# A transformer layer on eight cores: the second LayerNorm's rows turned into columns by DMAs instead of TensorE

## What is computed

```python
x = x + attn(layernorm(x))        # 16 heads of 128; causal; out @ out_w.T + out_b
x = x + ffn(layernorm(x))

def ffn(x):                       # gate_w, up_w: 2048 x 6144, down_w: 6144 x 2048, rounded to fp8
    gate = silu((x @ gate_w) * gate_scale)
    up = (x @ up_w) * up_scale
    return ((gate * up) @ down_w) * down_scale

def layernorm(x):
    return (x - mean(x)) / sqrt(var(x) + 1e-5)
```

## Time and profile before

| | us |
|---|---|
| median of 3 runs (1669.6 to 1670.41) | 1670.07 |
| the profiled execution | 1671.04 |
| its span on the slowest core (the cores: 1663.9 to 1669.5) | 1669.5 |
| TensorE busy | 1581.0 |
| VectorE busy | 477.4 |
| ScalarE busy | 377.7 |
| granted TensorE clock, mean | 0.995 |

### The profile page before, as it was taken

The page is one execution under the profiler, slowest core; times in us unless marked ns, Lnnn a source line. Parts: engine busy times, 40 slices in busy tenths (PEclk is TensorE's granted clock), DMA queues, the critical chain, the costliest instruction groups (busy, mean ns, idle before and its releaser), DMA issues.

```text
span 1669.5 us, 23252 instructions; the slowest of 8 cores (1663.9 to 1669.5 us)
## 1 busy us (share of the span) xinstructions
PE 1581.0 (95%) x8897; PEld 779.7 (47%) x9034; DVE 477.4 (29%) x1053; ACT 377.7 (23%) x508; POOL 65.9 (4%) x128
## 2 busy tenths in 40 slices
PE   3788999999998999999999999999999999999998
PEld 2544555555555544444444444444444444444444
DVE  5564455445445566111111111111111111111111
ACT  3453555555556311100000000000000000000000
POOL 0000000000000000000000000000000000000000
PEclk9899999999999999999999999999999999999999
DMA  9624325112143772535365646564444091939210
GB/s 301 173 72 77 61 51 96 20 30 33 20 68 65 114 214 89 101 31 45 33 56 47 53 37 54 49 52 38 38 39 38 1 109 55 98 79 106 79 52 29
DMA packets 33099, 117.15 MB, mean 70 GB/s; under 512 B 3744, under 2 KB 6112, under 8 KB 28128
## 3 DMA queue, kind: packets, MB, share of 16 engines
q0 software_dynamic: 17856, 58.73, 35.1%
q1 hardware_dynamic: 15136, 56.93, 10.5%
HBM read 233.08 MB, written 16.78 MB: 150 GB/s over the span
## 4 chain that ended last, share of the span: by engine, by line
PE 89%; DVE 4%; DMA 3%; issue 2%; ACT 1%; SPq 0%; DVEq 0%; ACTq 0%
PE PS L1083 20%; PE PS L1063 20%; PE PS L1069 20%; PE PS L890 7%; PE PS L1045 6%; PE PS L975 3%; PE PS L899 3%; PE PS L909 3%; PE PS L854 3%; PE PS L953 3%; DMA X<-xq 2%; PE PS L835 1%; DMA RES<-xq 1%; PE PS L934 1%; DVE ONa L600 1%
## 5 line engine op out<-in xcount | busy, mean ns | idle before, releaser
L1063 PE MATMUL PS<-X2T,W 128*128 128x512 bf16 x1506 | 344.9, 379 | 2.7 <-DVE RES L644 1.1
L1069 PE MATMUL PS<-X2T,W 128*128 128x512 bf16 x1505 | 344.9, 379 | 1.6
L696 DVE SCALAR_TENSOR_TENSOR FUSE<-PS,CF,SIL 128x512 bf16<-128x512 f32 x96 | 72.1, 751 | 589.8 <-PE PS L1069 581.3
L1063 PEld LDWEIGHTS PS<-X2T,W 128*128 128x128 fp8e4 x1536 | 150.1, 98 | 182.3 <-issue 1.5
L1069 PEld LDWEIGHTS PS<-X2T,W 128*128 128x128 fp8e4 x1536 | 150.3, 98 | 181.2
L771 ACT ACTIVATE P<-PS,NEGB 128x1024 bf16<-128x1024 f32 x192 | 172.3, 900 | 139.6 <-PE PS L953 137.0
L820 ACT ACTIVATE SIL<-PS,CF 128x512 bf16<-128x512 f32 x96 | 65.9, 687 | 584.7 <-PE PS L1063 584.7
L1083 PE MATMUL PS<-WDa,FUSE 128*128 128x512 fp8e4 x768 | 166.1, 379 | 1.2 <-DVE FUSE L696 1.2
L1083 PE MATMUL PS<-WDb,FUSE 128*128 128x512 fp8e4 x768 | 166.1, 379 | 0.0
L890 PE MATMUL PS<-XQT,WQ 128*128 128x512 bf16 x500 | 131.2, 379 | 0.9
L1083 PEld LDWEIGHTS PS<-WDa,FUSE 128*128 128x128 bf16 x768 | 75.0, 98 | 92.1 <-issue 1.7
(11 more groups left out here) (128 smaller groups left out, 1058.0 us busy)
## 6 DMA issues: line engine op xcount, KB each, us to landing
W<-gu POOLq DMA_DIRECT2D x48, 512.0 KB, 9.5
X<-xq SPq DMA_DIRECT2D x8, 1024.0 KB, 10.3
X<-xo SPq DMA_DIRECT2D x8, 1024.0 KB, 5.5
WQ<-wq POOLq DMA_DIRECT2D x16, 512.0 KB, 6.6
WO<-wo POOLq DMA_DIRECT2D x16, 512.0 KB, 10.0
RES<-xq SPq DMA_DIRECT2D x8, 1024.0 KB, 13.9
res_scr<-RES SPq DMA_DIRECT2D x8, 1024.0 KB, 5.5
RB<-res_scr SPq DMA_DIRECT2D x32, 256.0 KB, 4.4
```

The source lines that it names most:

```text
L696: e.scalar_tensor_tensor(FUSE[:, io * 1024 + qb * 512:io * 1024 + qb * 512 + 512], bank(2 * (f % 3) + 1), USC[:, io:io + 1], SIL[f % 3][:, ...
L1063: mm = e.matmul(bank(2 * (f % 3)), W8[io % 4][:, c * 128:(c + 1) * 128], X2T[:, c * 1024 + qb * 512:c * 1024 + qb * 512 + 512], start=(c = ...
L1069: mm = e.matmul(bank(2 * (f % 3) + 1), W8[io % 4][:, 2048 + c * 128:2048 + (c + 1) * 128], X2T[:, c * 1024 + qb * 512:c * 1024 + qb * 512 ...
```

## The change

The 16 groups of transposes into banks 6 and 7, ScalarE's copies of them, and their place in the list of banks go. The sync queue issues one transposing DMA for each tile, XH2 (128 x 2048, bf16) straight into X2T, when VectorE has written XH2, with a semaphore for each of the two buffers (`d_turn`). Its list is rewritten: four RES loads first, then for each tile the write to res_scr, the transposing DMA, and for the first four tiles a wait for that write and the load of RES for tile t + 4. VectorE waits for `d_turn` before it overwrites an XH2 buffer. FFN job 0 waits for 30 adds and for the turns of tiles 0 to 3, job 1 for 32 adds, job 2 for all turns. The down projection begins at 92 products, asks for 94 at the 47th matmul of its first output tile, and for 96 at its fifth.

```diff
--- before.py
+++ after.py
@@ -236,6 +236,7 @@
     d_idb = sem("d_idb")
     d_outb = sem("d_outb")
     d_dsc = sem("d_dsc")
+    d_turn = [sem("d_turn0"), sem("d_turn1")]
     d_wkva = [sem(f"d_wkva{i}") for i in range(4)]
     d_wq = [sem(f"d_wq{i}") for i in range(3)]
     d_wk = [sem(f"d_wk{i}") for i in range(2)]
@@ -307,7 +308,6 @@
             order += [(job, 6 + job[2] % 2 if job[0] == "P" else 6 if job[0] in "QNXY" else 7)
                       for job, lo, _ in st if lo == 0]
     order += [(("P", 0, 2), 6), (("P", 0, 3), 7), (("O", 15, 1), 6)]
-    order += [(("T", 16 + t, half), 6 + half) for t in range(8) for half in range(2)]
     BANK = dict(order)
     assert len(BANK) == len(order)
     BEFORE = {}
@@ -395,25 +395,25 @@
             load_x(n)
         e.wait_ge(v_latt, 16)
         e.dma_start(out=OUTB[:, :], in_=A(outb_d, 0, [[0, 128], [1, 2048]])).then_inc(d_outb, 16)
-        for t in range(8):
-            if t < 2:
-                e.wait_ge(t_q, count(("Q", 15, 1)))
-                e.wait_ge(t_k, count(("K", 15, 3)))
-            elif t < 4:
+        def load_res(t):
+            e.dma_start(out=RES[t % 4][:, :], in_=xq_d.ap()[t * 128:(t + 1) * 128, :]).then_inc(d_r[t % 4], 16)
+
+        e.wait_ge(t_q, count(("Q", 15, 1)))
+        e.wait_ge(t_k, count(("K", 15, 3)))
+        for t in range(4):
+            if t == 2:
                 e.wait_ge(t_av, 192)
                 e.wait_ge(t_o, 32)
-            else:
-                e.wait_ge(d_spill[t % 4], 16 * (t // 4))
-                e.wait_ge(v_xh, 16 + t - 3)
-            e.dma_start(out=RES[t % 4][:, :], in_=xq_d.ap()[t * 128:(t + 1) * 128, :]).then_inc(d_r[t % 4], 16)
-            if t >= 2:
-                e.wait_ge(v_add, 4 * (t - 1))
-                e.dma_start(out=res_d.ap()[(t - 2) * 128:(t - 1) * 128, :],
-                            in_=RES[(t - 2) % 4][:, :]).then_inc(d_spill[(t - 2) % 4], 16)
-        for t in range(6, 8):
+            load_res(t)
+        for t in range(8):
             e.wait_ge(v_add, 4 * (t + 1))
-            e.dma_start(out=res_d.ap()[t * 128:(t + 1) * 128, :],
-                        in_=RES[t % 4][:, :]).then_inc(d_spill[t % 4], 16)
+            e.dma_start(out=res_d.ap()[t * 128:(t + 1) * 128, :], in_=RES[t % 4][:, :]).then_inc(d_spill[t % 4], 16)
+            e.wait_ge(v_xh, 16 + t + 1)
+            e.dma_start_transpose(out=A(X2T, t * 128, [[16384, 128], [1024, 16], [1, 128]]),
+                                  in_=XH2[t % 2][:, :]).then_inc(d_turn[t % 2], 16)
+            if t < 4:
+                e.wait_ge(d_spill[t % 4], 16)
+                load_res(t + 4)
         for i in range(4):
             e.wait_ge(d_spill[i], 32)
         e.wait_ge(v_xh, 24)
@@ -423,7 +423,8 @@
             if m >= 4:
                 e.wait_ge(v_out, m - 3)
             else:
-                e.wait_ge(t_t, 48)
+                for i in range(2):
+                    e.wait_ge(d_turn[i], 64)
             e.dma_start(out=RB[m % 4][:, :],
                         in_=res_d.ap()[t * 128:(t + 1) * 128, db * 512:(db + 1) * 512]).then_inc(d_rb[m % 4], 16)
             if m >= 3:
@@ -683,7 +684,7 @@
             e.wait_ge(s_sd, 16 + t + 1)
             chain(e.reciprocal(RSTD[:, t % 8:t % 8 + 1], SD[t % 2][:, 0:1]))
             if t >= 2:
-                e.wait_ge(t_t, count(("T", 16 + t - 2, 1)))
+                e.wait_ge(d_turn[t % 2], 16 * (t // 2))
             e.tensor_scalar(XH2[t % 2][:, :], r[:, :], MV[t % 4][:, 0:1], RSTD[:, t % 8:t % 8 + 1],
                             Op.subtract, Op.mult).then_inc(v_xh, 1)
             if t < 7:
@@ -719,10 +720,8 @@
                 e.wait_ge(t_t, count(job))
                 if n < 8:
                     out = A(XQT, half * 8 * 1024 + n * 128, [[16384, 128], [1024, 8], [1, 128]])
-                elif n < 16:
+                else:
                     out = A(XOT[n // 4 - 2][half], (n % 4) * 128, [[4096, 128], [512, 8], [1, 128]])
-                else:
-                    out = A(X2T, half * 8 * 1024 + (n - 16) * 128, [[16384, 128], [1024, 8], [1, 128]])
                 e.activation(out, bankb(ring(job)), AFT.Identity).then_inc(s_t, 1)
 
         def lat_out(tb, dl):
@@ -812,7 +811,6 @@
         evict(("O", 15, 1))
         for t in range(8):
             sqrt_var(16 + t)
-            transposed(16 + t)
         for f, (io, qb) in enumerate(FFN):
             e.wait_ge(t_g, f + 1)
             if f >= 3:
@@ -1045,18 +1043,19 @@
                     mm = e.matmul(bank(d), OT[:, c * 1024 + t * 128:c * 1024 + (t + 1) * 128],
                                   WO[c][:, d * 512:(d + 1) * 512], start=(c == 0), stop=(c == 15))
                 mm.then_inc(t_p, 1)
-                if d == 1:
-                    transposes(16 + t - 1, XH2[(t - 1) % 2])
 
         for f, (io, qb) in enumerate(FFN):
             if qb == 0:
                 e.wait_ge(d_gu[io % 4], 16 * (io // 4 + 1))
             if f == 0:
+                e.wait_ge(v_add, 30)
+                for i in range(2):
+                    e.wait_ge(d_turn[i], 32)
+            if f == 1:
                 e.wait_ge(v_add, 32)
             if f == 2:
-                e.wait_ge(s_t, 48)
-            if f < 2:
-                e.wait_ge(s_t, 40)
+                for i in range(2):
+                    e.wait_ge(d_turn[i], 64)
             if f >= 3:
                 e.wait_ge(s_silu, f - 2)
             for c in range(16):
@@ -1069,17 +1068,19 @@
                 mm = e.matmul(bank(2 * (f % 3) + 1), W8[io % 4][:, 2048 + c * 128:2048 + (c + 1) * 128],
                               X2T[:, c * 1024 + qb * 512:c * 1024 + qb * 512 + 512], start=(c == 0), stop=(c == 15))
             mm.then_inc(t_u, 1)
-            if f == 0:
-                transposes(23, XH2[1])
-
-        e.wait_ge(v_fuse, 96)
+
+        e.wait_ge(v_fuse, 92)
         for m in range(32):
             db, t = divmod(m, 8)
+            if m == 4:
+                e.wait_ge(v_fuse, 96)
             if t == 0:
                 e.wait_ge(d_dn[db % 2], 96 * (db // 2 + 1))
             if m >= 2:
                 e.wait_ge(v_out, m - 1)
             for c in range(48):
+                if m == 0 and c == 46:
+                    e.wait_ge(v_fuse, 94)
                 mm = e.matmul(bank(6 + m % 2), FUSE[:, c * 1024 + t * 128:c * 1024 + (t + 1) * 128],
                               WD[db % 2][:, c * 512:(c + 1) * 512], start=(c == 0), stop=(c == 47))
             mm.then_inc(t_d, 1)
```

## The result

The changed kernel takes 1660.92 us (median) against 1669.84 us before; the ratio is 0.9943, with a 95% interval of 0.9924 to 0.9963. The forecast was 1661 us, 9.4 us less than before. Medians here are over all runs; ratios and their intervals leave out nearly all executions that a lower granted clock on one die made longer.

A forecast was written before the change was run, and what follows sets the result against it. TensorE, busy for 95% of the span, was taken as the bound. Gains of 7.1 + 1.1 + 1.2 = 9.4 us, less 0 to 0.4, from 1670.07 gave 1661 us; range 1659.8 to 1695, the forecast's own 1659.8 to 1663.

The forecast's parts named there:

- Transposes off TensorE: Output projection: eight groups of 16 transposes leave TensorE's chain, 0.89 us each, 7.1 us in all.
- The two finer waits: TensorE's gaps before the FFN and before the down projection go, gaining 1.08 and 1.2 us.
- D: Time one 512 KB transposing DMA holds the DMA engines: taken as 1.3 to 4.1 us, with 10 us the other end.
- (b): Third FFN job waits for tile 7's transposing DMA: 9.6 us remain for it, so 1.3 to 4.1 us fit.
- (a): XH2 writer of tile 2 waits for tile 0's transposing DMA: stall D - 3.7 us if positive, 0 to 0.4 forecast.
- (c): Sync queue: per tile 5.4 + D us against 13.8 of TensorE, 4 us of cover for the reload, cost 0.
- microseconds in issuing: Sign that the forecast is wrong: the sync queue busy for microseconds in issuing one transposing DMA.
- landings under 6 us once the engines are free: Sign for the forecast in the changed kernel's trace: transposing DMAs land that fast when the DMA engines are free.
- The slow rival: Transposing DMAs bound the sync queue before the third FFN job; slower from D = 7.5, 1693 us at 10.0; chance 0.30.
- a part is given back: D of 4.1 to 6.7 us, or tile 0's DMA late beside converting loads: 1663 to 1665 us; chance 0.13.
- The pages: Skill pages on transposing DMAs: one gives D as 1.3 to 1.5 us, the other's block time an estimate of 20.9 us.

The follow-up runs named there:

- `e1_turns_only`: The changed kernel with the three coarse waits of before put back, so the transposing DMAs alone: 1663.18 us, ratio 0.9967.
- `e2_waits_only`: The kernel before with only the FFN's and down projection's first waits made finer, transposes still on TensorE: 1667.96 us beside 1670.31, ratio 0.9995.
- `e4_turn_twice`: The changed kernel with each tile's transposing DMA followed by a second one into unused SBUF: 1660.45 us, ratio 0.9939.
- `e5_last_x4`: The changed kernel with the last tile's transposing DMA sent four times in a row, each after the landing of the one before: 1670.83 us, ratio 0.9998.
- `e6_act_queue`: The changed kernel with the transposing DMAs issued on ScalarE's queue, loads and writes staying on the sync queue: 1661.38 us, ratio 0.9945.
- `e8_turn_and_three`: The changed kernel with three more copies after each transposing DMA, each waiting for the landing of the one before: 1721.4 us, ratio 1.0307.
- `e3_gu_late`: The changed kernel with GpSimd's first four converting FFN weight loads held back until XH2 of tile 3 is written: 1688.38 us, ratio 1.0063.
- `e7_first_four`: The changed kernel with tiles 12 to 15 of the first LayerNorm also turned by transposing DMAs on the sync queue: 1665.66 us, ratio 0.9971.
- `e11_first_four_held`: `e7_first_four` with GpSimd's four converting weight loads waiting until its four transposing DMAs have landed: 1658.59 us, ratio 0.9929.

## Why the prediction was right, step by step

- *Transposes off TensorE, 7.1 us.* Right: 0.89 us per tile in the chain, and 7.1 us between 1670.3 and 1663.2 (`e1_turns_only`).
- *The two finer waits, 1.1 and 1.2 us.* Right: both gaps gone, 2.3 us together by `e1_turns_only`, 2.4 by `e2_waits_only`. Nothing took their place.
- *D from 1.3 to 4.1 us.* Right by the engines' time: its queue held the engines for 64.2% of 6 us, 3.9 us with the end of the write and the beginning of the next load among them, nearly all of turn 7's pieces went out in the 2.4 us from 664.6 (the last line shown in this section), and `e4_turn_twice` shows that twice as many turns fit.
- *(b), the last turn.* From its issue to the third job it was 672.75 - 663.37 = 9.4 us, where 9.6 were forecast; less a landing of 4.3 that left 5.1 us of cover. `e5_last_x4` measured it: three more landings of some 4.3 us made 8.0 us of wait, so 4.9 to 5.1 us were free.
- *(a), turn 0 lands at 597.3 + D and must by 601.* It landed at 595.7 and TensorE did not wait. In the changed kernel the reason held too. The DMA views from 567 to 592 and from 592 to 596 us:

```profile
DMA packets 776, 4.37 MB, mean 175 GB/s; under 512 B 73, under 2 KB 73, under 8 KB 415
...
DMA packets 2139, 0.82 MB, mean 205 GB/s; under 512 B 2103, under 2 KB 2103, under 8 KB 2103
```

  Turn 0's 2080 packets stood behind the loads and the write of their queue, the write landed at 593.9 (563.49 + 30.4), and then they went out at once. The forecast had the transfers ahead land at 597.3, so they gave 3.4 us of room that it had not counted on. What it did not see is that another queue would have brought nothing: in `e6_act_queue` the converting loads held turn 0 back until the same date.
- *(c), the sync queue at 0 us.* The cost was 0, but I had counted its transfers and not its issues. The issue of a turn held the queue for 25.95 us in tile 0 and 8.2 to 9.6 in the next four; the write of tile 1 went out at 594.41, though its last add was done at 576.33 + 0.69 = 577.0. The text named "microseconds in issuing" as a sign that the forecast was wrong. That sign came true and the forecast held, because nothing behind it on the queue was needed sooner. Another sign, landings under 6 us once the engines are free, came true for tiles 5 to 7 alone: tiles 1 to 4 took 10.4 to 12.1 us with the converting loads over, behind 2 MB of their own queue.
- *The slow rival.* It didn't come about. Its form was right: with a tile's queue time against 13.8 us of TensorE's, `e8_turn_and_three` kept the pace that was counted for its queue. Its point of decision was put into D alone. `e3_gu_late` shows turns that hold the queue for 21 to 47 us beside converting loads; the forecast named such sharing under "a part is given back", for turn 0 only, and gave it no size. In the changed kernel GpSimd issues none between 558 and 680 us, so turns 1 to 7 met none; the forecast had said only that the DMA engines are mostly free after 615 us.
- *The pages.* The page "Advanced Engine Details and Errata" of the Trainium skill, section "X-Bar Transpose (TRN2)", has transposing DMAs as fast as ordinary ones, at 350-400 GB/s. The trace doesn't bear it out even for one alone: 4.3 us to landing, beside 3.9 for a write of twice the bytes (tile 6, issued at 646.17), and 211 GB/s from 664.6 to 667 us, against 392 in the rows of before:

```profile
DMA packets 1988, 0.51 MB, mean 211 GB/s; under 512 B 1988, under 2 KB 1988, under 8 KB 1988
```

  D was some 2.5 us for it, and not 1.3 to 1.5. Of the page "VectorE: DVE Perf Modes" of the Trainium skill, section "The three transpose paths", 1309 ns for one block of 128 is no rate: 16 blocks landed in 4.3 us.

## What to carry to other kernels

Work that a saturated TensorE does for layout is worth its full time when a DMA can do it, and the price is not its bytes but its landing: ask what else is on the DMA engines in the microseconds between the tile's writing and its use, converting loads above all, and large loads of another queue, and leave on TensorE the tile that is needed within some 5 us. The issue of a turn can hold its queue until what is ahead of it has landed, so put behind it only what can wait. A wait of TensorE that is long enough to lower its clock costs more than its length.

## What the hardware showed that I had not expected

- A transposing DMA of 512 KB alone: 4.3 us to landing, 1.8 us of issue. Beside four converting loads: 28 us (tile 0, on either queue), 9.4 us (tile 15 of the first LayerNorm), 50.7 us at worst (`e3_gu_late`, tile 4). Its 256-byte packets get no more than a packet's place for each large one of another queue: 76, 78 and 76 from three queues in 5 us (`e6_act_queue`), 55 beside 69 in 2 us (`e7_first_four`), and holding the loads back repaired it (`e11_first_four_held`). The near standstill of `e3_gu_late` isn't explained by this: there 405 packets of the sync queue and 16 of the converting loads moved in 10 us.
- A load without conversion on another queue does it too: with 0.9 us between the issues a turn landed after 13.9 and 14.8 us, with 1.6 or more after 4.4 (`e6_act_queue`).
- Its issue is not done in a fixed time: 1.84 to 25.95 us in the changed kernel, 46.72 us in `e3_gu_late`, where the issues of ordinary DMAs around it took 0.33 to 1.1. It ended with the landing of what was ahead on its queue in the changed kernel, but tile 3's turn in `e3_gu_late` was held for 20.96 us with nothing ahead; what sets the length there is open.
- After 8.0 us without work TensorE's granted clock was 0.50 and was back at 0.95 in the five microseconds after that; this added 1.7 us to the stall in `e5_last_x4`. After 6.5 us in `e7_first_four` it was 0.56; after 1.32 us in `e11_first_four_held` it was still 1.00.
